# Values of two steps of the eight-head attention issued one after the other, and exponentials kept in a ring of three steps

## What is computed

```
# block 3: attention with one head over the 1024 pixels
alpha = softmax(einsum('bci,bcj->bij', q, k) * C ** -0.5)
x = x + conv1x1(einsum('bcj,bij->bci', v, alpha), wp, bp)
# block 4: attention with 8 heads of 16 channels
attn = softmax(einsum('bhdi,bhdj->bhij', q, k) * temp)
out  = einsum('bhdj,bhij->bhdi', v, attn)
x = x + conv1x1(out, w_out, b_out);  y = group_norm(x)
return x + mlp(y)
```

## Time and profile before

| | us |
|---|---|
| median of 3 runs | 1871.0 |
| lowest, highest | 1866.97, 1877.07 |
| the profiled execution | 1865.36 |
| its span (first to last instruction) | 1863.9 |
| PE busy, share of the span | 1565.3, 84% |
| DVE busy | 1133.5, 61% |
| ACT busy | 815.9, 44% |
| mean granted clock of TensorE | 0.871 |

### The profile page before, as it was taken

The page is one execution under the profiler, slowest core; times in us unless marked ns, Lnnn a source line. Parts: engine busy times, 40 slices in busy tenths (PEclk is TensorE's granted clock), DMA queues, the critical chain, the costliest instruction groups (busy, mean ns, idle before and its releaser), DMA issues.

```text
span 1863.9 us, 20833 instructions
## 1 busy us (share of the span) xinstructions
PE 1565.3 (84%) x6466; PEld 695.4 (37%) x6466; DVE 1133.5 (61%) x1912; ACT 815.9 (44%) x1514; POOL 273.7 (15%) x305
## 2 busy tenths in 40 slices
PE   6579679898889989899889998799879989985982
PEld 3236325433443335333343335333343334332330
DVE  5454664766568584767568574776667574665601
ACT  1113202465327552465327552365326553752670
POOL 5004102110130103010130102201130103000000
PEclk6789957998889799899889799898899899976995
DMA  2000012011110303011120303003020203023001
GB/s 50 12 12 6 11 29 52 6 26 45 28 37 7 80 1 65 6 29 53 25 41 7 80 1 60 12 7 75 12 53 7 68 11 61 18 52 58 13 12 35
DMA packets 31569, 58.64 MB, mean 31 GB/s; under 512 B 14678, under 2 KB 16862, under 8 KB 31456
## 3 DMA queue, kind: packets, MB, share of 16 engines
q1 hardware_dynamic: 27296, 50.41, 12.6%
q0 software_dynamic: 4160, 6.83, 2.4%
HBM read 14.37 MB, written 4.50 MB: 10 GB/s over the span
## 4 chain that ended last, share of the span: by engine, by line
PE 52%; issue 20%; DVE 8%; DMA 6%; SPq 5%; ACT 4%; POOL 3%; POOLq 0%; ACTq 0%; DVEq 0%
PE ps L1337 52%; SPq L689 3%; DVE x L1189 3%; DVE mx L1283 3%; DMA invw<-inverse_sums 2%; DMA qp<-q3h 2%; POOL acc L849 2%; ACT p L1015 2%; SPq L666 1%; SPq L692 1%; POOL ogc L816 1%; DMA inverse_sums<-inv 1%; ACT hn L928 0%; DVE x L1196 0%; DVE x L1195 0%
## 5 line engine op out<-in xcount | busy, mean ns | idle before, releaser
L1283 DVE TENSOR_REDUCE mx<-ps 128x1 f32<-128x512 f32 x1024 | 648.8, 682 | 259.6 <-PE ps L1337 257.5
L1015 ACT ACTIVATE p<-ps 128x512 f32<-128x512 f32 x1024 | 550.7, 600 | 304.6 <-PE ps L1337 302.5
L1337 PE MATMUL ps<-kp,qp 63*128 63x512 f32 x1024 | 418.2, 512 | 85.2 <-DVE mx L1283 41.4
L1337 PE MATMUL ps<-qp,kp 64*128 64x512 f32 x1024 | 396.5, 478 | 22.5 <-ACT p L1015 17.7
L1337 PEld LDWEIGHTS ps<-qp,kp 64*128 64x128 f32 x1024 | 172.3, 198 | 330.0 <-ACT p L1015 233.5
L1337 PE MATMUL ps<-p,vt 128*32 128x512 f32 x2048 | 287.9, 635 | 6.5 <-ACT p L1015 6.2
L1337 PEld LDWEIGHTS ps<-kp,qp 63*128 63x128 f32 x1024 | 176.2, 206 | 216.8 <-DVE mx L1283 133.8
L980 ACT ACTIVATE p<-ps 128x512 f32<-128x512 f32 x128 | 76.2, 597 | 220.5 <-PE ps L1337 188.3
L1337 PE MATMUL ps<-p,vT 128*128 128x512 f32 x256 | 143.5, 654 | 0.7 <-ACT p L980 0.5
L849 POOL TENSOR_TENSOR acc<-acc,p 128x512 f32<-128x512 f32 x96 | 126.4, 1316 | 70.8 <-ACT p L980 67.3
L1279 DVE TENSOR_REDUCE mx<-ps 128x1 f32<-128x512 f32 x128 | 84.4, 683 | 39.1 <-PE ps L1337 39.1
(11 more groups left out here) (192 smaller groups left out, 1660.3 us busy)
## 6 DMA issues: line engine op xcount, KB each, us to landing
qp<-q3h SPq DMA_DIRECT2D x128, 64.0 KB, 2.9
xin<-in_x SPq DMA_DIRECT2D x8, 512.0 KB, 4.6
acc<-inverse_sums SPq DMA_DIRECT2D x16, 256.0 KB, 3.7
kp<-k3h POOLq DMA_DIRECT2D x64, 64.0 KB, 4.1
qp<-q3l SPq DMA_DIRECT2D x64, 64.0 KB, 3.2
x3a<-x SPq DMA_DIRECT2D x8, 512.0 KB, 4.7
kp<-k3h SPq DMA_DIRECT2D x64, 64.0 KB, 2.5
x3b<-x3a SPq DMA_DIRECT2D x8, 512.0 KB, 2.9
```

What stands on the lines that cost most here:

```text
L1015: a.activation(p3[:, s % 2, i, :], ps[:, SB + (u + 1) % 3, :], ACT.Exp).then_inc(sem("p3_ready"), 1)
L1283: v.tensor_reduce(mx3[:, i, c, h:h + 1], ps[:, bank, :], AX.X, ALU.max).then_inc(sem("mx3_ready"), 1)
L1337: return nc.tensor.matmul(o, l, r, start=start, stop=stop)
```

## The change

1. The values of two steps are issued together. In lap 1 of the even steps s = 2, 4, ..., 16, PE makes the four products of step s-2 and right behind them the four of step s-1; the odd steps have none. Each step still raises `pv3_done` once.
2. `p3` has `RING = 3` steps, and step n of the image (0 to 31) lies in slot n % 3. The first exponential of step n waits for the values of step n-3.
3. `p2` is no tile of its own: it is the third slot of `p3`. So the first exponential of step 2 waits until the one-head attention has been multiplied and added up (`pv2_done`, `acc_steps`), and the first exponential of the one-head attention waits for the values of step 29 of the image before.
4. The tables move some work by a lap or a few: in `STEADY` the 16 tiles of maxima of the one-head attention end at lap 82 (before at lap 86), the turn of their result on DVE stands at lap 83 (before 87), the steps of `TL` stand a lap earlier; in `FIRST` two filler products (`keep_clock`) are put at laps 9 and 10.

The diff, cut to its core:

```
+RING = 3
-        p2 = sb("p2", [128, 4, HALF])
-        p3 = sb("p3", [128, 2, GH, HALF])
+        p3 = sb("p3", [128, RING, GH, HALF])
+        p2 = p3[:, RING - 1, :, :]
...
+                elif u == 0:
+                    wait(act, sem("pv3_done"), bt + -2, NG * STEPS, NG * STEPS - 2)
...
-                            if i == 0 and step >= 2:
-                                wait(act, sem("pv3_done"), bt, NG * STEPS, step - 1)
+                            if i == 0 and step >= RING:
+                                wait(act, sem("pv3_done"), bt, NG * STEPS, step - RING + 1)
+                            elif i == 0 and step == RING - 1 and attention:
+                                wait(act, sem("pv2_done"), bt + 1, A2_TILES)
+                                wait(act, sem("acc_steps"), bt + 1, (NC - 1) * NH)
                             elif i == 0:
-                                wait(act, sem("pv3_done"), bt + -1, NG * STEPS, NG * STEPS - 1 + step)
+                                wait(act, sem("pv3_done"), bt + -1, NG * STEPS, min(NG * STEPS, NG * STEPS - 1 + step))
-                            a.activation(p3[:, s % 2, i, :], ps[:, SB + (u + 1) % 3, :], ACT.Exp).then_inc(sem("p3_ready"), 1)
+                            a.activation(p3[:, step % RING, i, :], ps[:, SB + (u + 1) % 3, :], ACT.Exp).then_inc(sem("p3_ready"), 1)
...
-                        if heads and 0 <= q < HEAD_LAPS and i == 1 and s:
-                            h, j = divmod(s - 1, NC)
+                        if heads and 0 <= q < HEAD_LAPS and i == 1 and s and s % 2 == 0:
+                            h, j = divmod(s - 2, NC)
...
-                            for k in range(GH):
-                                last = mm(ps[32 * k:32 * (k + 1), VB, :], vt3[g][:, j, k, :], p3[:, (s - 1) % 2, k, :],
-                                          start=j == 0, stop=j == NC - 1)
-                            last.then_inc(sem("pv3_done"), 1)
+                            for j in (j, j + 1):
+                                step = g * STEPS + NC * h + j
+                                for k in range(GH):
+                                    last = mm(ps[32 * k:32 * (k + 1), VB, :], vt3[g][:, j, k, :], p3[:, step % RING, k, :],
+                                              start=j == 0, stop=j == NC - 1)
+                                last.then_inc(sem("pv3_done"), 1)
... (STEADY)
-              "000000000000000000000000000000000000000000000000000000000000001010000110111102120100011000000000...
+              "000000000000000000000000000000000000000000000000000000000000001100000100111202120210000000000000...
-    "turned": {"DVE": (69, 87, 157), "PE": (71, 87, 157), "ACT": (71, 89, 158), "SP": (72, 90, 158)},
+    "turned": {"DVE": (69, 83, 157), "PE": (71, 87, 157), "ACT": (71, 89, 158), "SP": (72, 90, 158)},
```

More of the change, by code:

```diff
@@ L55 @@
     "tiles": ("000000000000000000000000000000000000000000000001101101101101101101101100000000000000000000000000000000000000000000000000000000000000000000000000000000000000000000000000000000000000000000000000000000000000000000000000000000000",
-              "000000000000000000000000000000000000000000000000000000000000000000000000000000000000000000000000000000000000000000000000000000000110100000100010011001101112110000000000000000000000000000000000000000000000000000000000000000000",
+              "000000000000000000000000000000000000000000000000000000000000000000000000000000000000000000000000000000000000000000000000000000000100101000100001001100201112110000000000000000000000000000000000000000000000000000000000000000000",
               "000000000000000000000000000000000000000000000000000000000000000000000000000000000000000000000000000000000000000000000000000000000000000000000000000000000000011111111111111111111111111111111111111111111111111111111111111110000"),
@@ L133 @@
     "tiles": ("000000002222211500102111111111011100111111111111102111121111110011111000000000000000000000000000000000000000000000000000000000000000000000000000000000000000000000000000000000000000",
-              "000000000000000000000000000000000000000000000000000000000000001010000110111102120100011000000000000000000000000000000000000000000000000000000000000000000000000000000000000000000000",
-              "000000000000000000000000000000000000000000000000000000000000000000000000000000000000000000001031111111011111111111111111111111111112101111111111110110211111100000000000000000000000"),
-    "turned": {"DVE": (69, 87, 157), "PE": (71, 87, 157), "ACT": (71, 89, 158), "SP": (72, 90, 158)},
+              "000000000000000000000000000000000000000000000000000000000000001100000100111202120210000000000000000000000000000000000000000000000000000000000000000000000000000000000000000000000000",
+              "000000000000000000000000000000000000000000000000000000000000000000000000000000000000000000001031111111011111111111111111111012111112101111111111110110211111100000000000000000000000"),
+    "turned": {"DVE": (69, 83, 157), "PE": (71, 87, 157), "ACT": (71, 89, 158), "SP": (72, 90, 158)},
     "moved": (82, 110),
@@ L166 @@
             "Q3": {4: 47},
-            "TL": {8: 89},
+            "TL": {8: 88},
             "L0": {26: 148},
@@ L174 @@
             "Q3": {0: 0},
-            "TL": {15: 98},
-            "L0": {0: 98, 18: 132},
+            "TL": {15: 97},
+            "L0": {0: 97, 18: 132},
             "HN": {0: 1, 2: 3, 3: 4},
@@ L239 @@
             "L0": {0: 98, 18: 132},
-            "HN": {0: 1, 2: 3, 3: 4},
+            "HN": {0: 3, 2: 3, 3: 4},
         },
```

## The result

| | before | after |
|---|---|---|
| median | 1868.99 us (4 runs) | 1921.97 us (4 runs, 1916.87 to 1924.47) |
| span of the profiled execution | 1863.9 us | 1923.0 us |
| mean granted clock of TensorE | 0.871 | 0.864 |

The change makes the kernel slower by 2.9%: ratio 1.0287, 95% interval 1.0256 to 1.0318. The prediction was 1865, within 1843 to 1884. The median of before has one execution more than the 1871.0 ahead of the prediction. Two executions of this document, one of the kernel before and one of split_pair, stood at mean clocks of 0.543 and 0.655 and took 2341 and 2129 us; the ratios leave them out.

The account below looks back on a forecast made before the run. It took PE as the bound in steps with side chains, a PE-ACT loop in those without, and packing between groups; -21 + 12 + 7 - 3 - 1 = -6 gave 1859, scaled by 1.003 to 1865 us, range 1843 to 1884.

Parts of the forecast that it names:

- What bounds the kernel now: Steps with side chains: PE; without: a loop of PE and ACT, 2.67 us a step; between groups: the packing wait.
- (a): Steps with side chains: joining saves PE 0.32 us between scores, about 3.4 us a full window, -21 us in all.
- The price of the pair: The second group of a joined pair of values on PE costs 0.88 us; a join saves 0.32 between scores.
- (b): Group 1's first values move from inside the packing wait to behind it, 1.7 us in windows 0 to 6, +12 us.
- (c): Steps without side chains: two steps take 5.6 us instead of 5.34, 27 pairs at 0.26, +7 us.
- (d): Clock rises earlier behind the border in about half of windows 1, 3, 5 and 6, -3; start filler, -1 us.
- (e): New waits of the three-step ring and shared `p2`, and the moved table entries, lie under cover and cost nothing.
- The second one: The longer PE block starves ACT and DVE in steps with side chains too: +11 us, 1882 us, chance 0.16.
- The first rival: PE is the bound nearly everywhere and the pair raises the clock early at every border: -25 us, 1846, chance 0.37.

Follow-up runs that it names:

- split_pair: Changed kernel with the tables of before and the second group of values two laps behind the first, except at each half's end: 1927.7 us, ratio 1.0317.
- join_old_tables: Changed kernel with the tables of before (maxima, tail and filler where they stood): 1939.0 us, ratio 1.0383 to the kernel before.
- join_g0_only: Changed kernel with values joined in group 0 alone, group 1 and the tables as before: 1902.8 us, ratio 1.0201 to the kernel before.
- first_apart: join_old_tables with the values of group 1's first two steps standing alone again, in lap 1 of the next step: 1923.4 us, ratio 1.0322.
- ring_only: Kernel before, its tables and order of values kept, with only the ring of three and the shared `p2`: 1865.6 us, ratio 1.0001.
- new_tables_single: Kernel before with the tables of the changed one and nothing else: 1861.7 us, ratio 0.9989.
- late_lap: Kernel before with ring of three and each step's single values in lap 2 of the next step, except each half's last: 1884.4 us, ratio 1.0124.

## Why the prediction was wrong

- **What bounds the kernel now.** Right for the border. Too simple for steps with side chains, as (a) tells. Wrong for most steps without side chains: I took one loop of PE and ACT from the last window for all of them. More than half of them also make maxima, and there DVE is busy for 2.48 of 2.74 us.
- **The price of the pair.** Right: 0.86 for the second group, 0.88 forecast, 128 pairs of 16 records.
- **(a), -21 us: the step that failed.** It priced the change by what PE saves, and took the missing waits of one step as proof that PE would have nothing to wait for once its work came in lumps. PE was the bound there only because its work was even: with it in lumps, ACT and DVE set the step without values and PE the one with two groups. The saving exists: steps 11 and 12 of group 0, windows 0 to 4, 8.21 us before and 8.03 in join_old_tables, steps 13 and 14 8.89 and 8.77, so 0.12 to 0.18 a pair where 0.32 was forecast. Against it stand 1.4 us lost in steps 9 to 14 of each group 1, in the same windows. And joined in group 0 alone, join_g0_only is 2.0% slower, not faster. What is left of the 59 us for this step, when the others below are taken out, is +14 instead of -21 (59 - 11 - 9 - 21 - 4); this is a remainder of estimates and not a measurement.
- **(b), +12 us.** Right in place and in the sum, 11 us in steps 0 to 2 of group 1 (join_old_tables less first_apart), but the sum by luck: 0.75 in each of windows 0 to 4 where 1.7 was forecast, 1.9 and 0.8 in windows 5 and 6, and 4.4 in window 7, which the forecast did not count.
- **(c), +7 us.** Near in size by luck: 0.15 a pair in steps without maxima (0.26 forecast) and 0.5 in those with them, an estimate of 12 and 15 pairs, so +9. It asked for what ACT has in its banks alone and never held the pair against DVE's own 2.48 us.
- **(d), -3 and -1 us.** Wrong in sign. I asked only what a pair does where the clock is low, and not what the steps between pairs do where it is high, though the prediction named just this as what would make it wrong. Up to +21.
- **(e), waits that cost nothing.** Right for the ring and the shared slot: ring_only is 1.0001. The moved table entries were put there too, at nothing, and the places between the groups grew by 4 us (by 2 in new_tables_single, which as a whole loses nothing).
- **The rivals.** The second one, that the longer block starves ACT and DVE, had the direction and too small a price (1882, chance 0.16): it asked about the block of 2 us and not about the step of 4 us without values behind it. split_pair, which has no block of two but at a half's end, keeps the loss (1.0317): the block is the smaller part. The first rival (1846, 0.37) rested on the same missing wait as (a).

## What to carry to other kernels

Here the engines exchange tiles through a ring shorter than one step. The saving by grouping the busiest engine's work was paid back: the other engines set the steps without that work, the busiest one those with it. Before joining, write down for each engine the least time of a step with and without the moved work (here ACT 1.9, DVE 2.5, PE 1.0 more) and add the larger of each; a mean busy share of 0.84 says nothing of it. And look for what a late piece was hidden behind: one group of values moved past the border cost 2 us each time in late_lap.

## What the runs showed of the hardware

I had not expected the clock to fall while PE is shown busy for nine tenths of the time, with no wait of a microsecond in the 6.8 us before. Products on all 128 rows in the steps between (two of 0.23 us each) kept it at the higher level, with one such product the heads had 181 us at the lower level instead of 143. And the mean clock is not set by the amount of work alone: join_old_tables and the changed kernel do the same work in the same full-clock time (1659 and 1661) and differ by 17 us in the median. late_lap shows the same from the other side: 21 us over the kernel before, at an equal full-clock time (1629 and 1629).
